# A tokenizer bias moved from TensorE to VectorE, and five steps of the routing put elsewhere inside the attention stage

## What is computed

```
h = tokenizer(x)                      # 16x16 patches @ W + b, layernorm, * gamma + beta
h = h + attention(layernorm(h))       # 16 heads of 64, rope, causal softmax, @ Wo + bo
h = h + moe(layernorm(h))             # router softmax, top 2 of 4 experts, silu(x w1) * (x w3) @ w2
h = h + recurrence(layernorm(h))      # complex decay per feature
out = h + quantised_ffn(layernorm(h)) # fake-quantised gated ffn
```

## Time and profile before

| | us |
|---|---|
| median of 3 runs (lowest, highest) | 1851.52 (1844.16, 1861.87) |
| the profiled execution's own time | 1846.75 |
| its span (first to last instruction) | 1845.0 |
| PE, DVE, ACT, POOL busy | 1569.1, 1234.4, 993.0, 1012.3 |
| granted TensorE clock, mean | 0.936 |

### The profile page before, as it was taken

The page is one execution under the profiler, slowest core; times in us unless marked ns, Lnnn a source line. Parts: engine busy times, 40 slices in busy tenths (PEclk is TensorE's granted clock), DMA queues, the critical chain, the costliest instruction groups (busy, mean ns, idle before and its releaser), DMA issues. The chain is left out here.

```text
span 1845.0 us, 31424 instructions
## 1 busy us (share of the span) xinstructions
PE 1569.1 (85%) x11349; PEld 1457.6 (79%) x11349; DVE 1234.4 (67%) x2511; ACT 993.0 (54%) x2138; POOL 1012.3 (55%) x814
## 2 busy tenths in 40 slices
PE   7759999999999999999669999999998846699229
PEld 4449998888888888888669999999997836598129
DVE  2637677676767677667525666666668759558896
ACT  2636575656656565656345545555544424449562
POOL 2557676776858594959256776776665633100000
PEclk9959999999999999999879999999999978799659
DMA  6282101001000000000055555555544331003223
GB/s 213 77 287 87 35 3 34 19 18 35 18 30 24 26 27 24 13 18 19 30 187 165 147 139 141 141 135 150 136 131 126 90 82 43 26 1 126 83 67 110
DMA packets 86130, 150.46 MB, mean 82 GB/s; under 512 B 7992, under 2 KB 63608, under 8 KB 85720
## 3 DMA queue, kind: packets, MB, share of 16 engines
q1 hardware_dynamic: 75464, 134.62, 23.4%
q0 software_dynamic: 10512, 13.83, 4.4%
HBM read 111.88 MB, written 49.91 MB: 88 GB/s over the span
## 5 line engine op out<-in xcount | busy, mean ns | idle before, releaser
L1525 POOL TENSOR_TENSOR expert_w_low<-expert_raw,expert_w_high 128x768 fp32r<-128x768 f32 x152 | 288.5, 1946 | 174.1 <-ACT expert_w_high L1350 169.1
L827 ACT ACTIVATE expert_raw<-psum,neg_max 120x376 f32<-120x376 f32 (+2 forms) x384 | 176.3, 482 | 102.1 <-DVE neg_max L988 102.0
L656 PE MATMUL psum<-diag,expert_raw 128*128 128x128 f32 (+2 forms) x1536 | 200.5, 281 | 11.8 <-DVE pt_low L1004 11.8
L951 POOL TENSOR_TENSOR rotated<-expert_raw 128x376 f32<-128x376 f32 x128 | 128.2, 1002 | 134.7 <-ACT expert_raw L814 119.6
L1004 DVE TENSOR_TENSOR pt_low<-psum,pt_high 128x752 fp32r<-128x752 f32 x128 | 120.5, 941 | 118.5 <-ACT pt_high L836 117.3
L656 PEld LDWEIGHTS psum<-diag,expert_raw 128*128 128x128 f32 (+2 forms) x1536 | 182.8, 192 | 18.6 <-ACT expert_raw L814 11.5
L1497 DVE TENSOR_TENSOR expert_act_low<-expert_act,expert_act_high 128x384 fp32r<-128x384 f32 x152 | 140.2, 922 | 79.5 <-ACT expert_act_high L1388 79.5
L1388 ACT ACTIVATE expert_act_high<-expert_act 128x384 fp32r<-128x384 f32 x152 | 79.8, 525 | 203.9 <-DVE expert_act L1492 203.9
L1309 PE MATMUL psum<-slots_high,expert_w_high 128*128 128x384 f32 x608 | 160.3, 345 | 18.9 <-DVE expert_act L1492 17.7
L927 POOL TENSOR_TENSOR qk_low<-rotated,qk_high 128x376 fp32r<-128x376 f32 x128 | 136.1, 1063 | 60.9 <-ACT qk_high L820 58.9
L1309 PE MATMUL psum<-slots_low,expert_w_high 128*128 128x384 f32 x608 | 156.9, 339 | 0.0
(11 more groups left out here) (297 smaller groups left out, 4450.0 us busy)
## 6 DMA issues: line engine op xcount, KB each, us to landing
expert_raw<-in_experts SPq DMA_DIRECT2D x152, 384.0 KB, 3.1
x_slots<-in_c_slots SPq DMA_DIRECT2D x4, 3168.0 KB, 29.2
slot_rows<-x_slots SPq DMA_DIRECT2D x19, 396.0 KB, 4.6
up_spill<-held SPq DMA_DIRECT2D x5, 1128.0 KB, 5.0
held<-up_spill SPq DMA_DIRECT2D x5, 1128.0 KB, 5.7
attn_x<-tok_xt SPq DMA_DIRECT2D x6, 752.0 KB, 4.0
x_parts<-attn_x SPq DMA_DIRECT2D x6, 752.0 KB, 4.7
patch<-in_patches SPq DMA_DIRECT2D x8, 376.0 KB, 7.2
```

Source lines behind the costliest of these rows:

```text
L656: last = pe.matmul(psum[0:nj, BANK_PT + bank, at:at + ni], probs[0:ni, h % 2, src:src + nj], diag[0:ni, h % 2, it, 0:ni], start=True, stop ...
L827: last = act.activation(probs[0:ni, h % 2, at:at + P * it + ni], score_bank(h % 2, it), ACT.Exp, bias=neg_max[0:ni, h % 2, it:it + 1], acc ...
L951: pool.tensor_tensor(rotated[:, k, :], raw[:, k, :], cos[:], ALU.mult).then_inc(rope_made, 1)
L1525: pool.tensor_tensor(w[1][:, g % RING, :], raw[:, g % RAW, :], w[0][:, g % RING, :].bitcast(F32), ALU.subtract).then_inc(w_low, 1)
```

## The change

It has six parts, by code. (1) In the tokenizer the bias products on PE go; DVE adds the bias row from the bank into a new tile `tok_y` (`biased`), waits for itself, and takes the statistics there; ACT scales out of `tok_y`; PE may refill a bank after `y_made`, and no longer waits for the rows of constants. (2) The six scatters of a batch stand after n = 5 (two), 7, 9, 11 and 13 (one each). (3) `scale_rows` does one of its three passes in each of steps 0, 1 and 2. (4) `out_high` goes ahead of `qk_split(ahead)` on ACT. (5) `keep_turned` and `weigh` go ahead of `turned_high(2c+1)` and `turned_low(2c+1)`. (6) `choose` stands between the second and the third residual.

```diff
 # tokens_in
-        one_row = sb("tok_ones", [P, P])
+        y = sb("tok_y", [P, 2, T, DIM])
                     if b >= 2:
-                        pe.wait_ge(h_scaled, b - 1)
+                        pe.wait_ge(y_made, b - 1)
                     for k in range(T):
                         n = TILE_ROWS[k]
-                        pe.matmul(tok_bank(b)[0:n, k, :], one_row[0:1, 0:n], per_col[0:1, 0, :], start=True, stop=False)
                         for c in range(2):
                             last = pe.matmul(tok_bank(b)[0:n, k, :], patch[:, c, TOK * b + P * k:TOK * b + P * k + n],
-                                             w[:, c, :], start=False, stop=(c == 1))
+                                             w[:, c, :], start=(c == 0), stop=(c == 1))
...
                 pe.wait_ge(w_in, 16)
-                pe.wait_ge(rows_in, 16)
-                pe.wait_ge(prepared, 3)
...
-                        last = act.activation(h[0:n, b % 3, k, :], tok_bank(b)[0:n, k, :], ACT.Identity,
+                        last = act.activation(h[0:n, b % 3, k, :], y[0:n, u, k, :], ACT.Identity,
...
+                def biased(b):
+                    u, n = b % 2, TILE_ROWS[2]
+                    dve.wait_ge(tok_made, b + 1)
+                    if b >= 2:
+                        dve.wait_ge(h_scaled, b - 1)
+                    dve.tensor_tensor(y[:, u, 0:2, :], tok_bank(b)[:, 0:2, :],
+                                      per_col[:, 0:1, :].broadcast_to((P, 2, DIM)), ALU.add)
+                    ins = dve.tensor_tensor(y[0:n, u, 2, :], tok_bank(b)[0:n, 2, :], per_col[0:n, 0, :], ALU.add)
+                    ins.then_inc(y_made, 1)
+                    dve.wait_ge(y_made, b + 1)
...
+                dve.wait_ge(rows_in, 16)
                 for i in range(BATCH + 4):
                     if here(i):
-                        dve.wait_ge(tok_made, i + 1)
-                        stat(0, i, tok_bank(i))
+                        biased(i)
+                        stat(0, i, y[:, i % 2, :, :])
 # attention
-        SCATTER_AT = (6, 8, 10)
+        SCATTER_AT = {5: ((0, 0), (0, 1)), 7: ((1, 0),), 9: ((1, 1),), 11: ((2, 0),), 13: ((2, 1),)}
 # ACT, step
-                    turned_high(b, 2 * c + 1)
                     if b and c in ROUTE_X:
                         keep_turned(b - 1, ROUTE_X.index(c))
+                    turned_high(b, 2 * c + 1)
...
                         raw_copy(b, ahead + 1)
+                    out_high(b, c)
+                    if projects:
                         qk_split(b, ahead)
-                    out_high(b, c)
-                    if b and c == 1:
-                        scale_rows(b - 1)
+                    if b and c < T:
+                        scale_rows(b - 1, (c,))
 # POOL, loop over n
                         if b >= 2 and n in SCATTER_AT:
-                            scatter(b - 2, (SCATTER_AT.index(n),))
+                            scatter(b - 2, SCATTER_AT[n])
 # DVE, begin
-                    if b >= 2:
-                        choose(b - 2)
...
                             add_bo(b - 1)
-                            for k in range(T):
-                                residual(b - 1, k)
+                            residual(b - 1, 0)
+                            residual(b - 1, 1)
+                            if b >= 2:
+                                choose(b - 2)
+                            residual(b - 1, 2)
 # DVE, step
-                    turned_low(b, 2 * c + 1)
                     if b and c == ROUTE_LOGITS:
                         weigh(b - 1)
+                    turned_low(b, 2 * c + 1)
```

More of the change, by code:

```diff
@@ L114, in tokens_in @@
         summed, std_made, rstd_made = ([sem(f"tok_{n}{i}") for i in range(2)] for n in ("summed", "std_made", "rstd_made"))
-        (w_in, rows_in, tok_made, h_scaled, h_gained, h_made, x_made, x_turned, x_high, x_kept, w_high, w_low_dve,
+        (w_in, rows_in, tok_made, y_made, h_scaled, h_gained, h_made, x_made, x_turned, x_high, x_kept, w_high, w_low_dve,
          w_low_pool, step, decayed, rooted, prepared, cleared, tables_in) = (
             sem(f"tok_{n}") for n in
-            "w_in rows_in tok_made h_scaled h_gained h_made x_made x_turned x_high x_kept w_high w_low_dve "
+            "w_in rows_in tok_made y_made h_scaled h_gained h_made x_made x_turned x_high x_kept w_high w_low_dve "
             "w_low_pool step decayed rooted prepared cleared tables_in".split())
@@ L344, in _ @@
                     dve.memset(moments[i][:], 1.0).then_inc(prepared, 1)
-                dve.memset(one_row[:], 1.0).then_inc(prepared, 1)
                 dve.memset(tables["ones_b"][:], 1.0)
                 dve.memset(rows[:], 0.0)
-                dve.wait_ge(prepared, 3)
+                dve.wait_ge(prepared, 2)
                 first_turns()
+                dve.wait_ge(rows_in, 16)
                 for i in range(BATCH + 4):
                     if here(i):
-                        dve.wait_ge(tok_made, i + 1)
-                        stat(0, i, tok_bank(i))
+                        biased(i)
+                        stat(0, i, y[:, i % 2, :, :])
                     if here(i - 4):
@@ L846, in deviation, with scale_rows @@
                                    bias=consts[:, EPS_LN:EPS_LN + 1]).then_inc(std_made, 1)
-                def scale_rows(b):
+                def scale_rows(b, tiles):
                     act.wait_ge(rstd_made, b + 1)
@@ L851, in scale_rows @@
                         act.wait_ge(scattered[b % 2], 32 * T * (b // 2))
-                    for k in range(T):
+                    for k in tiles:
                         n = TILE_ROWS[k]
@@ L913, in _ @@
                 deviation(LAST)
-                scale_rows(LAST)
+                scale_rows(LAST, range(T))
                 keep_turned(LAST, 0)
@@ L928, in qk_split, with scatter @@
                                        qk[0][:, c % 2, k, :].bitcast(F32), ALU.subtract).then_inc(qk_ready, 1)
-                def scatter(b, tiles):
+                def scatter(b, pieces):
                     u = b % 2
@@ L936, in scatter @@
                     pool.wait_ge(x_made, T * (b + 1))
-                    for k in tiles:
+                    for k, j in pieces:
                         n = TILE_ROWS[k]
[L939 to L942, removed]
+                        pool.indirect_dma_start(
+                            x_slots, bass.IndirectOffsetOnAxis(ap=slots_u[0:n, u, j, k:k + 1], axis=0),
+                            rows[0:n, u, k, :], None).then_inc(scattered[u], 16)
                 for part in range(2):
@@ L959, in _ @@
                         if b >= 2 and n in SCATTER_AT:
-                            scatter(b - 2, (SCATTER_AT.index(n),))
+                            scatter(b - 2, SCATTER_AT[n])
                 qk_split(LAST, 2 * PAIRS - 1)
                 for b in (LAST - 1, LAST):
-                    scatter(b, range(T))
+                    scatter(b, [(k, j) for k in range(T) for j in range(2)])
                 for u in range(2):
```

## The result

| us | before | after |
|---|---|---|
| median (lowest to highest), 4 runs each on one chip | 1849.14 (1844.16 to 1861.87) | 1788.53 (1788.23 to 1790.23) |
| span of the profiled execution | 1845.0 | 1786.5 |
| first projection of attention starts | 110.3 | 89.6 |
| from there to the last mixing product | 793.0 | 758.2 |
| from there to the end | 941.7 | 938.7 |

The ratio is 0.9664, with a 95% interval of 0.9614 to 0.9714: faster by 60.6 us, where 40 were forecast. Of the 58.5 us of the span, the tokenizer gives 20.7 (predicted 11), attention 34.8 (predicted 29), and 3.0 lie behind the last mixing product. These 58.5 are 18.5 more than the 40 of the forecast: 9.7 of them in the tokenizer, 5.8 in attention, 3.0 in that last stretch.

What follows compares the result with a forecast made beforehand. PE was taken to set the pace in attention and, until 60 us, in the tokenizer, with DVE after. Attention 29 plus tokenizer 11 gave 40 off 1846.75, so 1807 on the profile's scale; forecast 1808, range 1792 to 1834 us.

Steps and rivals of the forecast that it cites:

- Part 1: Tokenizer: without bias products a batch's PE work takes 6.2 us instead of 9.4, DVE's add costs 1.1; 11 us gained.
- third rival: Tokenizer: PE's clock rises in the first batches without one-row products; batch 7 some 7 us earlier, 1800 us; chance 0.08.
- the 0.8 kept for the range: Tokenizer: DVE's bias add might also wait for a whole POOL operation, 0.8 us more, making 1.9 instead of 1.1.
- Parts 2 to 4: Attention, per batch: single scatters leave 0.7 of 1.5 us of `qk_low` waits; split scaling and earlier `out_high` remove all 1.7.
- nearly the passes' length: Attention: three scaling passes (1.57 us) stand before `pt_high`, and PE's 1.74 wait was read as nearly their length.
- Part 5: Attention, per batch: earlier bank reads remove the 0.9 us wait for odds whole and leave 0.45 of `router_x`'s 0.9.
- Part 6: Attention, per batch: the first residual no longer queues behind `choose`, so its 1.0 us wait goes, at no cost.
- The sum in attention: Attention: 4.8 us gained in each of batches 2 to 6, 2.2 in batch 1, 2.5 in the last; 29 in all.
- Attention did not give half: Rival for attention: POOL stretches beside DVE and scaling passes are paid, 15 us less gain, 1823 us; chance 0.24.
- the tokenizer did not give little: Rival for the tokenizer: DVE's add costs 1.9 us, gain falls from 11 to 7, 1812 with late first load; chance 0.10.
- POOL's queue was not blocked by the pair behind n = 5: Rival for attention: the scatter pair waits for late slot numbers and holds up POOL's in-order queue; slower, 1867 us; chance 0.03.
- what would show it: Signs: tokenizer's last statistics near 68; no `odds`, `attn_h` or 1.7 `pt_low` wait, `qk_low` under 1, batches 4.8 us sooner.

Runs made afterwards that it cites:

- without part 5: The kernel after with the bank reads put back behind the turned rows, all else kept: 1796.59 us, ratio 0.9706 to before.
- before plus part 2: The kernel before with only the scatters changed, to a pair after n = 5 and then single ones: 1829.48 us, ratio 0.9908 to before.
- one of them on zeros: The kernel after with a one-row product of zeros put back ahead of each tile's patch products, bias still on DVE: 1816.01 us, ratio 0.9814 to before.
- the kernel with the 128-row bias: The kernel after with the tokenizer of before, its bias product on PE going over 128 rows instead of one: 1788.67 us, ratio 0.9657 to before.

## Why the prediction missed, point by point

**Part 1 failed, in the price of PE's product.** "So a batch takes 3 x 2.08 = 6.2 us" took the slow rows and dropped the one-row ones from them. In fact, without them the clock rose just behind batch 0, and batches 1 to 3 came after 3.2, 3.6 and 5.8 us instead of 6.2 each. The prediction had this as its third rival, at 0.08, with 7 us more gain. The mechanism was that rival's; the last statistics came 9.3 earlier than forecast. Against the forecast's own times the first statistics came 1.7 earlier (1.1 from the start, counted as zero, 0.6 from a batch 0 of 5.6 us), batches 1 to 3 gave 6.0, batch 4, with the clock low again, took back 1.6 (9.1 instead of 7.5), and the last three gave 3.1 (7.0 each, not 8.0). The add itself was right: 0.69 + 0.41 = 1.1 in all eight batches, with POOL busy beside it in five of them, so the 0.8 kept for the range was never paid. What misled was a reading of the earlier trace rows: the clock column said 1.00 for 10 to 60 while the 2.08 against 1.13 of the earlier trace rows said 1.2 GHz. The prediction saw both, and then took "it did not until 60" against the rival. But the one-row products were in that evidence, and they were what the change removed. The Trainium skill, "TensorE: Matmul & The Clock Gate", section "What's actually happening", says that the slow clock is the default and activity releases it. The runs agree for products over 128 rows, where it rose 6 us after the first, and not for a stream with one-row products in it, which was unbroken for 59 us without a rise.

**Parts 2 to 4: right total, by luck, with wrong owners.** What is left in a batch is 1.6 us (forecast 1.6): 0.4 for `pt_low` as said, and 1.2 for `diag` that the prediction did not name. But part 2 was put at 0.8 a batch and is worth 3.0, and parts 3 and 4 were put at 1.7 and are worth next to nothing. The step that failed is the reading of the 1.74 as "nearly the passes' length". A wait and an instruction of like length stood next to each other, and the idle time of ACT ahead of the passes (2.06 for `rotated`) was not read. That the last four scatters take up to 0.3 each from POOL showed nowhere as `qk_low`.

**Part 5** was right in the odds: 0.9 whole. `router_x` was counted as half of 0.9 gone; without part 5 only 0.4 of it is there, the other 0.5 was the scatters' doing. **Part 6** was put at 1.0 and is worth 0.8 a batch with the others in place, with a wait of 0.5: its wait in before plus part 2 is still 1.0, so which part takes the other half is open.

**The sum in attention** came out at 34.8 instead of 29 with the waits left as forecast. From first transposition to first transposition, batch 1 gained 3.6 us (forecast 2.2), batches 2 to 6 gained 5.4 to 5.6 each (4.8), and the last 3.9 (2.5). In the last, the single scatters alone give 3.8. In the middle batches the step that failed is the count of a wait at its own length: taking 4.7 us of waits away took 5.4 off a batch, since PE's busy time fell by 0.7 with the same products. Where these 0.7 come from is open. The clock is not it: in batches 5 to 7 of before it fell to 0.50 for some 3 us behind the wait of 1.74 (649 to 651 reads 0.50), in after it did not, yet batches 5 and 6 with that fall (99.49, 99.32) are as long as batches 3 and 4 without it (99.28 both).

**The other rivals.** Attention did not give half; the tokenizer did not give little; POOL's queue was not blocked by the pair behind n = 5, and no `qk_low` wait is left in after. Of "what would show it", all signs on attention came true, and the one on the tokenizer (near 68) came out at 59.

## What to carry to other kernels

Before pricing products that remain, see whether those that go were what held TensorE's clock, as the one-row products were here: compare one form's duration at two places in the trace, and do not trust the granted clock alone. When an instruction and a wait stand side by side with the same length, read the idle time in front of that instruction's engine first, and undo each part once, since a right total can hide wrong owners. An engine that queues DMA issues (POOL here, 1.3 us each) pays for them in everything that waits for its next result; here the wait showed on PE, behind ACT and DVE.

## What the hardware showed that was not expected

- At 1.2 GHz a pair of products on 1 row takes about as long as one on 128 rows (1.19 us for the first pair of either), but the clock stayed down with it: it rose at 16 us with 128 rows, and at 50 to 71 in the four traces with one-row products, one of them on zeros. In all four the rise came within 1 us behind a set of six transpositions (L188 in before), while other such sets (at 48.36 in before) raised nothing; what decides is open.
- The granted clock of a window reads 1.00 up to the first rise, though products go at 1.2 GHz there: 10 to 60 in before, 10 to 20 in after. Later falls to 0.50 are shown and agree with the durations. Up to the first rise the duration of a form is the only witness.
- The moment of the rise varies between executions of the same code. Under the attention of after, the tokenizer of before had the clock up by 50 us and lost it again at 64, 2 us behind a gap of 1.23 on PE; gaps of up to 2.02 cost the kernel with the 128-row bias nothing, so the gap is not shown to be the cause. Its first projection then came at 112.4 instead of 110.3. The times of the kernels with one-row products also lie further apart, which fits: before from 1843 to 1862, before with part 2 from 1826 to 1839, after from 1788 to 1790. The timeline on PE of that kernel:

```profile
50.37 1.13 PE L176 MATMUL psum<-tok_w,patch 128*128 128x256 f32 x4
...
62.57 0.69 PE L174 MATMUL psum<-tok_rows,tok_ones 1*128 1x256 f32 x2
...
65.97 2.08 PE L176 MATMUL psum<-tok_w,patch 128*128 128x256 f32 x4
```

- The same DVE product of two SBUF tensors takes 0.56 to 1.98 us, depending on what POOL does.
